# Attention on one core: values of two key tiles after eight S^T, text denominators on TensorE, S^T two tiles ahead

## The reference

```python
x = x + attention(layernorm(x), ctx) @ Wo + bo      # mask "trinity"
x = x + ffn(layernorm(x))                           # SiLU-gated, 1408 wide, fake-quantised to 8 bits

def trinity_mask(txt_tok, img_tok):
    img_img = (i < img_tok) & (j < img_tok) & (i // sit == j // sit)
    txt_img = (i >= img_tok) & (j < img_tok)
    txt_txt = (i >= img_tok) & (j >= img_tok) & (i >= j)
```

## Time and profile before

| what | us |
|---|---|
| median of three executions | 1152.42 (1151.9 to 1155.57) |
| the profiled execution, its own time | 1155.27 |
| its span, first to last instruction | 1153.5 |
| TensorE busy | 1062.2 (92%) |
| VectorE busy | 750.1 (65%) |
| GpSimd busy | 640.9 (56%) |
| ScalarE busy | 512.5 (44%) |
| mean granted TensorE clock | 0.951 |

### The profile page before, as it was taken

How to read it: one execution, slowest core, us unless ns; L and a number is a source line. 1 busy time by engine, 2 the same in 40 slices (tenths; PEclk the granted TensorE clock), 3 DMA queues, 4 the chain that set the end, 5 groups by cost and what they waited for, 6 DMA issues and landing times. The chain is left out here.

```text
span 1153.5 us, 18187 instructions
## 1 busy us (share of the span) xinstructions
PE 1062.2 (92%) x6527; PEld 704.8 (61%) x6550; DVE 750.1 (65%) x1340; ACT 512.5 (44%) x881; POOL 640.9 (56%) x345
## 2 busy tenths in 40 slices
PE   5999999999629989999999999899995799998898
PEld 4888888888516656666666666456763444443343
DVE  5665456654319757777777777236968477877785
ACT  3322223222101656666777666651110555553553
POOL 3434455344440979999999999555753113100373
PEclk9999999999955989999999999899997799999899
DMA  5987777856699896768888673449996353100876
GB/s 203 318 258 234 221 276 256 270 170 197 207 178 188 187 225 150 180 158 180 182 180 194 151 178 101 124 126 236 312 287 172 96 224 122 36 1 3 322 240 219
DMA packets 129619, 218.08 MB, mean 189 GB/s; under 512 B 29320, under 2 KB 55688, under 8 KB 128330
## 3 DMA queue, kind: packets, MB, share of 16 engines
q1 hardware_dynamic: 129546, 217.12, 68.1%
HBM read 134.76 MB, written 77.74 MB: 184 GB/s over the span
## 5 line engine op out<-in xcount | busy, mean ns | idle before, releaser
L775 ACT ACTIVATE a_probs<-a_banks 128x512 f32<-128x512 f32 (+2 forms) x512 | 233.9, 535 | 131.6 <-PE a_banks L991 106.6
L712 POOL TENSOR_TENSOR a_pair_sums<-a_probs,a_probs 128x2048 f32<-128x2048 f32 x48 | 223.6, 4658 | 66.3 <-ACT a_probs L775 57.6
L850 DVE TENSOR_REDUCE a_max<-a_banks 128x2 f32<-128x512 f32 x192 | 123.3, 685 | 53.8 <-PE a_banks L962 53.5
L991 PE MATMUL a_banks<-a_queries,a_keys 97*128 97x512 f32 x384 | 148.1, 429 | 10.4 <-ACT a_probs L775 5.7
L962 PE MATMUL a_banks<-a_keys,a_queries 96*128 96x256 f32 x384 | 86.0, 319 | 32.7 <-DMA a_queries<-q_split 32.7
L967 PE MATMUL a_banks<-a_keys,a_queries 96*128 96x512 f32 (+1 forms) x256 | 114.7, 462 | 0.0
L846 DVE CUSTOM_DVE_ANT_0 a_masked_scores<-a_banks,kept_mask 128x384 f32<-128x384 f32 (+1 forms) x128 | 79.5, 621 | 50.0 <-PE a_banks L967 49.7
L850 DVE TENSOR_REDUCE a_max_parts<-a_banks 128x1 f32<-128x512 f32 x128 | 87.9, 687 | 24.8 <-PE a_banks L967 20.9
L962 PEld LDWEIGHTS a_banks<-a_keys,a_queries 96*128 96x128 f32 x384 | 70.3, 205 | 54.5 <-DMA a_queries<-q_split 33.4
L1347 POOL TENSOR_TENSOR d_out<-d_out,f_x 128x512 f32<-128x512 f32 x28 | 42.6, 1548 | 99.1 <-DVE d_out L1375 99.1
L225 POOL TENSOR_SCALAR p_x<-p_x,p_neg_mean,p_rstd 128x512 f32<-128x512 f32 x32 | 28.2, 895 | 121.9 <-DVE p_rstd L330 121.9
(11 more groups left out here) (166 smaller groups left out, 2205.2 us busy)
## 6 DMA issues: line engine op xcount, KB each, us to landing
a_keys<-k_split SPq DMA_DIRECT2D x48, 512.0 KB, 8.5
a_queries<-q_split SPq DMA_DIRECT2D x48, 512.0 KB, 14.3
f_x<-x_scratch SPq DMA_DIRECT2D x14, 1024.0 KB, 7.8
p_c<-in_ctx_dram SPq DMA_DIRECT2D x8, 1024.0 KB, 8.8
p_x<-in_x_dram SPq DMA_DIRECT2D x8, 1024.0 KB, 10.9
v_scratch<-p_v_stage SPq DMA_DIRECT2D x16, 512.0 KB, 9.0
k_split<-p_stage_hi SPq DMA_DIRECT2D x16, 512.0 KB, 4.3
k_split<-p_stage_lo SPq DMA_DIRECT2D x16, 512.0 KB, 5.4
```

The costliest lines, as they stand in the source:

```text
L712: pool.tensor_tensor(PP[u % 2], PR[2 * c % 4], PR[(2 * c + 1) % 4], ALU.add).then_inc(paired, 1)
L775: act.activation(PR[kt % 4][:, j, 0:w], STB[:, n % NST, 0:w], ACT.Exp, scale=SCALE).then_inc(edone, 1)
L850: dve.tensor_reduce(out, src, AX.X, ALU.max).then_inc(wfree, 1)
L991: op = pe.matmul(out.rearrange("p (c t) -> p c t", t=SIT), keys, q, start=True, stop=True)
```

## The change

`AHEAD` goes from 3 to 2. GpSimd keeps the sum of each pair and the cut of the text tiles; its folds and the semaphores `folded` and `tden` go, and with them the waits on these. TensorE makes the text denominators in all groups as it did in groups 14 and 15. Values are made in the odd slots only, for tiles kt-1 and kt, followed by the text and the image denominators of the pair. The score pieces of a slot all go between its S^T, and the transpose of the maxima goes behind the S^T and pieces of slot 1; VectorE's `rows_out` moves accordingly.

```diff
--- before.py
+++ after.py
@@ -473,7 +473,7 @@
 S_ITEMS = 7
 S_PER_SLOT = (3, 3, 4, 4, 4, 3, 4, 3)
 TURN_SLOT = 1
-AHEAD = 3
+AHEAD = 2
 QROWS = 3 * DH
 NGRP = BATCH * G
 NST, NWK = 3, 3
@@ -548,8 +548,8 @@
         mready, nmready = s.sem("maxima"), s.sem("maxima_rows")
         stfull, edone, pvdone = s.sem("st_full"), s.sem("exp_done"), s.sem("pv_done")
         ifree, tfree = s.sem("image_free"), s.sem("text_free")
-        paired, folded, cutd = s.sem("probs_paired"), s.sem("text_probs_folded"), s.sem("probs_cut")
-        iden, tden = s.sem("image_denominators"), s.sem("text_denominators")
+        paired, cutd = s.sem("probs_paired"), s.sem("probs_cut")
+        iden = s.sem("pair_denominators")
         oout = [s.sem(f"out_stored{i}") for i in range(4)]
 
         ldw, ldb, whi, wsplit = s.sem("wo_loaded"), s.sem("bo_loaded"), s.sem("wo_hi_done"), s.sem("wo_split")
@@ -568,8 +568,6 @@
         LOADS = 6 * 16
         PIECES = [(j, m) for j in range(HG) for m in range(S_ITEMS)]
         NPC = len(PIECES)
-        FOLDS = 4
-        FOLDED = NGRP - 2
         OLOADS = 16 * (1 + HG)
         CHAIN = 3 + 4
         rows = lambda a, chunk: a.rearrange("(n t p) c -> n p t c", t=TT, p=P)[chunk]
@@ -707,25 +705,13 @@
                 pool.wait_ge(edone, HG * (NKT * i + 2 * c + 2))
                 if u >= 2:
                     pool.wait_ge(iden, u - 1)
-                if c == 1 and 0 < i <= FOLDED:
-                    pool.wait_ge(tden, i)
                 pool.tensor_tensor(PP[u % 2], PR[2 * c % 4], PR[(2 * c + 1) % 4], ALU.add).then_inc(paired, 1)
                 pool.wait_ge(paired, u + 1)
-                if c and i < FOLDED:
-                    text = PP[u % 2][:, :, SIT:]
-                    pool.tensor_tensor(text, text, PP[1 - u % 2][:, :, SIT:], ALU.add).then_inc(folded, 1)
-                    pool.wait_ge(folded, FOLDS * i + c)
-
-            def fold(i, kt):
-                w, n = N - kt * P, kt - IMG // P
-                probs, text = PR[kt % 4][:, :, 0:w], PP[(3 * i + 2) % 2][:, :, 512 - w:]
+
+            def cut(i, kt):
                 pool.wait_ge(edone, HG * (NKT * i + kt + 1))
                 pool.affine_select(out=PR[kt % 4][:, :, 0:P], in_=PR[kt % 4][:, :, 0:P], pattern=[[0, HG], [1, P]],
                                    base=0, channel_multiplier=-1, compare_op=ALU.is_ge, fill=0.0).then_inc(cutd, 1)
-                if i < FOLDED:
-                    pool.wait_ge(cutd, 2 * i + n + 1)
-                    pool.tensor_tensor(text, text, probs, ALU.add).then_inc(folded, 1)
-                    pool.wait_ge(folded, FOLDS * i + 3 + n)
 
             def divide(n):
 
@@ -745,8 +731,8 @@
                 for c in range(3):
                     pair(i, c)
                 for kt in range(IMG // P, NKT):
-                    fold(i, kt)
-                if i == FOLDED - 1:
+                    cut(i, kt)
+                if i == NGRP - 3:
                     pool.wait_ge(stfull, HG * NKT * (NGRP - 3))
                     pool.memset(f32(BIAS), 0.0).then_inc(bset, 1)
                     pool.memset(ONER, 1.0).then_inc(bset, 1)
@@ -766,8 +752,6 @@
                     act.wait_ge(pvdone, u - 3)
                     if was_kt < IMG // P:
                         act.wait_ge(paired, 3 * was_i + was_kt // 2 + 1)
-                    elif was_i < FOLDED:
-                        act.wait_ge(folded, FOLDS * was_i + 3 + was_kt - IMG // P)
                 w = sum(width(kt))
                 for j in range(HG):
                     n = HG * u + j
@@ -800,12 +784,9 @@
                         act.wait_ge(iden, 3 * i + kt // 2 + 1)
                         out_copy(kt // 2, IB, ifree, i)
                     if kt == NKT - 1:
-                        if i < FOLDED:
-                            act.wait_ge(tden, i + 1)
-                        else:
-                            act.wait_ge(pvdone, NKT * (i + 1))
+                        act.wait_ge(pvdone, NKT * (i + 1))
                         out_copy(3, TB, tfree, i)
-                    if i == FOLDED and kt == 1:
+                    if i == NGRP - 2 and kt == 1:
                         act.wait_ge(ldw, 16)
                         act.activation(WH, RAW, ACT.Copy).then_inc(whi, 1)
                         act.wait_ge(ldb, 32)
@@ -813,7 +794,7 @@
                         act.activation(BIAS[0:1], BR[0:1], ACT.Copy).then_inc(bhi, 1)
                         act.activation(BT[DH:DH + 1], BR[DH:DH + 1], ACT.Copy).then_inc(bhi, 1)
                         act.activation(ONE, ONER, ACT.Copy).then_inc(onec, 1)
-                    if i == FOLDED + 1 and kt == 4:
+                    if i == NGRP - 1 and kt == 4:
                         hi(0)
             hi(1)
             for n in range(NCH):
@@ -922,11 +903,11 @@
                 largest(1, k)
             for i in range(NGRP):
                 for kt in range(NKT):
-                    if kt == TURN_SLOT and i + 1 < NGRP:
-                        rows_out(i + 1)
                     if i + 2 < NGRP:
                         for k in slot_pieces(kt):
                             largest(i + 2, k)
+                    if kt == TURN_SLOT and i + 1 < NGRP:
+                        rows_out(i + 1)
                     if i > G and i % G == 1 and kt == 2:
                         invert(i // G - 1)
             dve.wait_ge(whi, 1)
@@ -1014,7 +995,7 @@
                                   skip_group_check=True)
                     op = pe.matmul(TB[rows, TXT - wt:TXT], v, p[:, j, wi:wi + wt], start=kt == 0,
                                    stop=kt == NKT - 1, skip_group_check=True)
-                if i >= FOLDED and not wi:
+                if not wi:
                     op = denominators(TB, p, slice(0, wt))
                 op.then_inc(pvdone, 1)
 
@@ -1067,21 +1048,18 @@
                     for j in range(HG):
                         if ahead:
                             score_t(u // NKT, u % NKT, j)
-                        if j == 1 and kt == TURN_SLOT and i + 1 < NGRP:
-                            turn_maxima(i + 1)
-                        if j and len(todo) > 1:
+                        if len(todo) >= HG - j:
                             scores(i + 2, todo.pop(0))
-                    values(i, kt)
-                    if kt in (1, 3, 5):
-                        pe.wait_ge(paired, 3 * i + kt // 2 + 1)
-                        if i >= FOLDED:
-                            denominators(TB, PP[(3 * i + kt // 2) % 2], slice(SIT, 512))
-                        denominators(IB, PP[(3 * i + kt // 2) % 2], slice(0, SIT)).then_inc(iden, 1)
-                    if kt == NKT - 1 and i < FOLDED:
-                        pe.wait_ge(folded, FOLDS * (i + 1))
-                        denominators(TB, PP[(3 * i + 2) % 2], slice(SIT, 512)).then_inc(tden, 1)
-                    for k in todo:
-                        scores(i + 2, k)
+                    if kt == TURN_SLOT and i + 1 < NGRP:
+                        turn_maxima(i + 1)
+                    if kt % 2:
+                        for k in (kt - 1, kt):
+                            values(i, k)
+                        if kt < IMG // P:
+                            pe.wait_ge(paired, 3 * i + kt // 2 + 1)
+                            for bank, cols in ((TB, slice(SIT, 512)), (IB, slice(0, SIT))):
+                                op = denominators(bank, PP[(3 * i + kt // 2) % 2], cols)
+                            op.then_inc(iden, 1)
             pe.wait_ge(wsplit, 1)
             for m in range(NCH):
                 pe.wait_ge(olo, m + 1)
```

## The result

| | before | after |
|---|---|---|
| median of four runs each | 1153.54 us (1151.9 to 1155.57) | 1179.34 us (1175.93 to 1179.58) |
| ratio after to before | | 1.0207, 95% interval 1.0188 to 1.0227 |
| profiled execution, its span | 1155.27, 1153.5 | 1179.58, 1177.8 |
| mean granted TensorE clock | 0.951 | 0.949 |

The account below looks back on a forecast made before the run. TensorE was taken to bound the kernel at 24.30 us a group. The terms 15.5 + 2.8 - 3 + 2.5 gave +17.8: 1155.27 to 1173 on the profiled execution, 1170 on the median, range 1160 to 1180.

Parts of the forecast that it names:

- step 7: Last two groups, from mark 722.03 to the last: 50.2 us against 47.71, so +2.5, bounds -1 and +5.
- What bounds it: Steady state: TensorE busy for all 24.30 us of a group, GpSimd for 23.49; dropping the folds gives nothing by itself.
- step 3: Three-bank rings of S^T (ScalarE) and pieces (VectorE) delay longer bursts: group 25.59 against 24.30, +15.5 us over 12 groups.
- The formulas of the rings: Earliest starts: S^T 3+k at mark + 1.84 + 0.49k, piece 3+k at the first piece + 1.19 + 0.61k.
- steps 1 and 2: TensorE per group: text denominators +1.5 us; four round trips fewer -1.36, four late fourth S^T fewer -0.4.
- the first rival: Rings don't bind, saved turns decide: a group takes 23.37 us, the kernel 1137; chance 0.13.
- step 4: VectorE's inversion, 0.94 us in slot 2 of groups 5, 9 and 13, between chained pieces: +2.8, bounds 0 and 2.8.
- step 5: GpSimd's pair sums, 4.66 us each, end before their denominators; the tightest, slots 0 and 1, hidden by 1.5 us.
- step 6: Start: TensorE's 4.64 us wait for group 2's shift rows is used up by work: -3, bounds -5 and 0.
- My third rival: A third wait, late pair sums or clock-lowering gaps: 1.5 us more a group, 12 groups, +18, 1188; chance 0.07.
- The second: Rival: only ScalarE's ring binds, VectorE's bursts start earlier than counted; group 24.07 us, kernel 1149; chance 0.10.

Follow-up runs that it names:

- The even pieces: Against the kernel after, seven score pieces behind each mark (start of the last small-matmul set before 128-column products) instead of 6, 8, 7, 7: 1169.38 us.
- the kernel with pairs and folds: Against the kernel after, GpSimd's folds and the single text set of groups 0 to 13 put back, values still two at a time: 1161.96 us.

## Why the prediction was right

The time moved as forecast, and 1179.34 lies at the upper edge of the range, 9 us over the likeliest value. The mechanism in steady state held; that the time stayed inside, with less than 1 us to spare, is partly luck, since step 7 came out beyond its own bounds. By steps:
- **What bounds it** held: the folds hid behind TensorE, and taking them off gave nothing; moved to TensorE they cost 1.51 us a group, which the run with no folds shows alone.
- **The two rings** (step 3) held to 0.1 us in every pair. The even pieces show VectorE's ring by an edit that changes no work; the releases of the last S^T show ScalarE's. What the rings take outweighs what is saved of the turns, 1.36 us by my prices, but only just: 0.12 us a group. A group came out at 25.70 against 25.59; over the middle, with the inversions, 18.75 was measured and 18.3 written. The Trainium skill, TensorEngine Tiling (Array Packing), Key Properties, says that changing the tiling mode drains TensorE. The 0.34 us of a round trip agree. The PSUM Bottleneck section of the same page of the Trainium skill says that emptying PSUM may become the limit once tiling has made TensorE faster. S^T 0.49 apart, released by ScalarE, agree.
- **Two slips** did not touch the forecast. The formulas of the rings should read 0.49(k-1) and 0.61(k-1): the fourth S^T, k = 1, stands at mark + 1.84, and the sums count it so. And steps 1 and 2 give an unhindered group of 24.30 + 1.5 - 1.36 - 0.4 = 24.04, step 3 gives 23.37: my prices leave some 0.7 us of a group of the kernel before unaccounted for, so the first rival's 23.37 was likely too low.
- **The inversion** (step 4): 0.82 each measured, 0.94 written.
- **Pair sums** (step 5) stayed hidden. With all folds they would not have: both kernels with two tiles ahead and all folds wait for GpSimd.
- **The start** (step 6): from the first transpose to the mark of group 2 the gain is 3.3 us, 3 written (its terms add up to mark 432.5, so 4), and the wait for the shift rows is gone.
- **The end** (step 7) is the mis-sized term: +2.5 written, within -1 and +5, and +8.85 measured. I allowed 3 us of half clock in one place, behind the split of `wo`, and there 3.1 is what its removal gave back in the kernel before; the profile after shows half clock in five places. My third rival named gaps that lower the clock, but put them in all groups, where the clock stays at 1.00. That the gaps are the cause is not shown: the same order, with the same gaps, mostly held the clock in the kernel with pairs and folds.
- The rest: about 1 us lies behind attention, within what that part varies by, and 2.6 come from the profiled executions, which lie 2.85 us over their median before and 0.24 after.

Of the rivals, the first (the saved turns decide) is out: with the same saving the group is longer. The second (only ScalarE's ring) is out by the even pieces and by the last piece at mark + 4.54.

## What to carry to other kernels

When work is gathered in longer bursts to save switches, count the banks: a ring of three lets a burst run free for three products, and from there the consumer's pitch decides, however idle the consumer is on average. A late engine off the path is worth relieving only if somebody waits for it, and a part of a change can depend on another: here two tiles ahead, slot by slot, cost 44 us with the folds, and without them a group became 0.23 us shorter. Look also at the end of a loop, where the other work runs out: the largest miss of the forecast lay there, and moving ScalarE's split of `wo` off that path gained 6 us in the kernel before.

## What was not expected of the hardware

- Two PSUM banks between TensorE and ScalarE lengthened ScalarE's pitch for 512 columns from 0.49 to 0.56 us (four in 2.28 instead of 2.07), though TensorE needs only 0.235 for its part.
- The same instructions of groups 14 and 15 took 56.6 us in one kernel and 48.9 in another, with the granted clock at 0.79 over the stretch in the first. Bursts with the same idle time of 0.30 us and the same pacing stood in both.
- In steady state of the kernel after, where pieces lie between S^T that are paced in the same way, the full clock (1.00) was kept throughout. Pieces are no safeguard by themselves: with two waits of 0.60 and 0.92 us a group (two tiles ahead alone) it fell to 0.88 in some groups.
